# Routing of a top-2 mixture of experts in two parts, the first inside the recurrence that feeds it

## The reference, cut to what matters

```python
x = x + _L0_ffn_ref(_L0_cond_ref(cond_1024, x, ...), ...)   # x: (32, 64, 256)
x = x + _L1_ffn_ref(_L1_cond_ref(x, cond_1024, ...), ...)

def step(h, z_t):                                  # L0_cond: 64 steps in a row
    gate = jax.nn.sigmoid(h @ Wh.T + z_t @ Wz.T + b)
    h_new = jnp.tanh(h * leak + gate * z_t)

gate_hidden = jnp.einsum('nh,erh->ner', x, W_A)    # L0_ffn: 2048 tokens, 8 experts
scores = jnp.sqrt(jnp.sum(gate_hidden * gate_hidden, axis=-1))
topk_scores, topk_idx = jax.lax.top_k(scores, K)   # K = 2
g = jnp.einsum('ner,efr->nef', gate_hidden, W_B)
up = jnp.einsum('nh,efh->nef', x, W_up)
y = jnp.einsum('nef,ehf->neh', jax.nn.silu(g) * up, W_down)
out = jnp.einsum('neh,ne->nh', y, w_full)          # w_full: softmax over the two chosen

h_next = jnp.tanh(xw_t + h_prev @ Wh)              # L1_cond: 64 steps; then L1_ffn: 256 -> 1024 -> 256, quantised
```

## Time and profile before

| | us |
|---|---|
| median of 3 runs | 438.21 (436.7 to 440.9) |
| the profiled execution | 437.36 |
| its span, first to last instruction | 435.6 |
| outside the span | 1.8 |
| PE busy in the span | 341.4 (78%) |
| DVE busy | 260.2 (60%) |
| ACT busy | 212.5 (49%) |
| POOL busy | 247.7 (57%) |

### The profile page before, as it was taken

How to read it: one execution, slowest core, us unless ns; L and a number is a source line. 1 busy time by engine, 2 the same in 40 slices (tenths; PEclk the granted TensorE clock), 3 DMA queues, 4 the chain that set the end, 5 groups by cost and what they waited for, 6 DMA issues and landing times.

```text
span 435.6 us, 12277 instructions
## 1 busy us (share of the span) xinstructions
PE 341.4 (78%) x3791; PEld 230.8 (53%) x3792; DVE 260.2 (60%) x758; ACT 212.5 (49%) x664; POOL 247.7 (57%) x274
## 2 busy tenths in 40 slices
PE   2478777778740179999999999999808999999982
PEld 1345444444410136666666666666507777677741
DVE  5246767767779746853443443343315788989781
ACT  2135555555541124444444445444323787787781
POOL 3579999999002466675445555552046677775231
PEclk9999999999985579999999999999976899999999
DMA  8972365616801012322232232233122122211011
GB/s 210 245 284 75 131 199 214 253 72 204 292 36 60 17 45 72 83 79 74 64 81 78 57 81 81 59 77 66 36 62 74 50 62 77 72 53 56 26 38 36
DMA packets 22525, 42.81 MB, mean 98 GB/s; under 512 B 3986, under 2 KB 14610, under 8 KB 21604
## 3 DMA queue, kind: packets, MB, share of 16 engines
q0 software_dynamic: 6560, 23.17, 18.0%
q1 hardware_dynamic: 15664, 19.31, 13.8%
q10 hardware_dynamic: 276, 0.01, 0.0%
HBM read 28.97 MB, written 13.50 MB: 97 GB/s over the span
## 4 chain that ended last, share of the span: by engine, by line
PE 53%; DVE 16%; DMA 10%; ACT 7%; issue 7%; POOL 2%; SPq 1%; DVEq 0%; POOLq 0%; ACTq 0%
PE bank L916 14%; PE bank L892 12%; DVE bank L1122 5%; PE bank L755 5%; PE bank L762 4%; DMA z<-x_fm 4%; PE bank L882 4%; PE bank L902 4%; DMA z_lo<-y_rows,idx 3%; ACT h_hi L576 2%; ACT bank L574 2%; DMA gate_rows<-ga_s 2%; PE bank L868 2%; PE bank L1020 2%; DVE wrec L1331 1%
## 5 line engine op out<-in xcount | busy, mean ns | idle before, releaser
L1265 DVE TENSOR_TENSOR wrec<-bank,wrec 128x512 f16<-128x512 f32 x39 | 27.0, 691 | 80.8 <-ACT wrec L636 80.6
L755 PE MATMUL bank<-h_hi,wrec_hi 128*128 128x32 f16 x512 | 43.7, 181 | 29.8 <-ACT h_hi L576 28.8
L892 PE MATMUL bank<-wup_s,xt 128*128 x234 | 64.4, 385 | 1.1 <-issue 1.1
L916 PE MATMUL bank<-wdn_s,wrec 128*128 x468 | 62.6, 278 | 3.0 <-ACT wrec L636 1.0
L755 PEld LDWEIGHTS bank<-h_hi,wrec_hi 128*128 128x128 f16 x512 | 34.5, 98 | 56.6 <-ACT h_hi L576 51.5
L478 POOL DMA_INDIRECT xs<-hs_rows,idx x39 | 41.5, 1065 | 31.6 <-POOL idx L474 31.6
L916 PEld LDWEIGHTS bank<-wdn_s,wrec 128*128 128x128 f16 x468 | 41.9, 96 | 17.2 <-issue 7.0
L630 ACT ACTIVATE z_lo<-bank 128x256 f32<-128x256 f32 x39 | 15.0, 384 | 61.6 <-PE bank L916 61.6
L481 POOL DMA_INDIRECT gs<-gate_rows,idx x39 | 38.2, 980 | 11.9 <-issue 11.3
L1122 DVE TENSOR_TENSOR_SCAN bank<-bank,terms 128x128 f32<-128x128 f32 x64 | 27.6, 432 | 28.6 <-ACT bank L574 24.9
L504 POOL DMA_INDIRECT z_lo<-y_rows,idx x32 | 32.3, 1009 | 18.1 <-POOL idx L499 12.2
(11 more groups left out here) (206 smaller groups left out, 922.4 us busy)
## 6 DMA issues: line engine op xcount, KB each, us to landing
y_rows<-z_lo SPq DMA_DIRECT2D x39, 128.0 KB
stage<-wup POOLq DMA_DIRECT2D x2, 2048.0 KB, 11.9
gate_rows<-ga_s SPq DMA_DIRECT2D x16, 256.0 KB, 2.7
stage<-wdn POOLq DMA_DIRECT2D x2, 2048.0 KB, 8.5
stage<-wb SPq DMA_DIRECT2D x2, 1024.0 KB, 13.6
hs_rows<-hs_out SPq DMA_DIRECT2D x16, 128.0 KB, 2.1
stage<-w POOLq DMA_DIRECT2D x2, 1024.0 KB, 7.5
stage<-x_tm POOLq DMA_DIRECT2D x1, 2048.0 KB, 16.0
```

The lines of the kernel that those rows point to most:

```text
L755: mm(fm(par)[:, ft, cols], w[:, m, kt, fcols], h_hi[pp][:, kt, pcols], start=False, stop=True, skip_group_check=True)
L892: ins = mm(bank[4 + par][:, :], xt[par][:, b, kt, :], w_slice(wup_s, a, kt, e), start=kt == 0 and n == 0, stop=kt == KT - 1 and n == 2)
L916: ins = mm(bank[6][:, 0:D], act_t[:, a, ft, :], w_slice(wdn_s, b, ft, e), start=n == 0, stop=n == len(todo) - 1)
L1265: ve.tensor_tensor(act_t[:, 1, :, :].rearrange("p k t -> p (k t)"), bank[(7, 3)[par]][:, :], act_t[:, 0, :, :].rearrange("p k t -> p (k t) ...
```

## The change

The token tiles are split in two parts, tiles 0 to 8 (`EARLY` = 9) and tiles 9 to 15.

The first part is routed during steps of the tiles 11 to 15 of the first recurrence; the last six tiles of it are now written out on PE and DVE. A slot is now known by expert and rank instead of by its place in one list. One-hot rows are made by small DVE instructions of 128 columns (`hots`, lines 1332 and 1333 of the new kernel), two for each token tile and choice, and PE inverts them by 128 x 128 products. Eighteen routed tile halves fill at least 11 slot tiles (`FIRST`), which form the front of the list. Their gathers need only the stored rows of tiles 0 to 8.

The second part is routed by DVE and PE between the expert tiles 0 to 7, and gives the 28 other slot tiles. The slots of the tokens, needed only for the last stage, are worked out at expert tiles 24 to 28. The mixing weights (square root and sigmoid on ACT) move to the last expert tile and behind it.

Gate rows are stored as 64 numbers in f32 instead of a high and a low half in f16. The split into halves is now made after the gather: PE transposes the f32 rows in one more f32 transpose (`transposed_in`), ACT copies both the rows and the high half of the gates (`copy_in`), and DVE forms the low half (`gates_low`). `copy_rows` in the recurrence moves from DVE to ACT, between the sigmoid and the tanh, in two halves. `v`, the scan's output, moves from PSUM bank 6 to bank 2, where `gate` already is.

The load of `x_tm` is issued behind the first two gathers. The constants that POOL makes (`iota`) move to the start of the program, and DVE waits for them before its first step. The work on the quantised weights on DVE is cut into quarters and spread over expert tiles 9 to 12 and 16 to 23. Expert tiles 1 to 16 are written out on PE.

```diff
@@ -23,6 +23,12 @@
 
 
 STILES = 2 * NTOK // P + E - 1
+
+FAR = 1000
+EARLY = 9
+FIRST = 2 * EARLY - E + 1
+CAP = NTOK // P
+COLS = E * CAP
...
+            gather_h(0, 0, EARLY * P)
+            gather_h(1, 1, EARLY * P)
+            pool.dma_start(rows, x_tm.rearrange("(t p) d -> p t d", p=P)).then_inc(s_restage[1], 16)
+            with pool.Fori(1, FIRST // 2) as i:
+                gather_h(2 * i, 0, EARLY * P)
+                gather_h(2 * i + 1, 1, EARLY * P)
+            gather_h(FIRST - 1, 0, EARLY * P)
+            pool.wait_ge(s_route, 2)
             pool.wait_ge(rows_st[0], 16 * TILES // 2)
             pool.wait_ge(rows_st[1], 16 * TILES // 2)
             pool.wait_ge(ga_st[0], 16 * TILES // 2)
             pool.wait_ge(ga_st[1], 16 * TILES // 2)
-
-            def gather_h(j, par):
-                if live(j - 2, STILES):
-                    pool.wait_ge(xt_mm, j - 1)
-                    pool.wait_ge(gh_mm, j - 1)
-                pool.tensor_copy(idx[par][:, 0:2], row_of_slot[:, bass.ds(j, 1), :].rearrange("p a c -> p (a c)")
-                                 ).then_inc(idx_ready, 1)
-                pool.wait_ge(idx_ready, j + 1)
-                pool.sem_inc(waited, 1)
-                pool.indirect_dma_start(out=xs[par][:, :], out_offset=None, in_=hs_dram,
-                                        in_offset=bass.IndirectOffsetOnAxis(ap=idx[par][:, 0:1], axis=0)
-                                        ).then_inc(gathered[par], 16)
-                pool.indirect_dma_start(out=gs[par][:, :], out_offset=None, in_=ga_dram,
-                                        in_offset=bass.IndirectOffsetOnAxis(ap=idx[par][:, 1:2], axis=0)
-                                        ).then_inc(gathered_g[par], 16)
-
-            gather_h(0, 0)
-            gather_h(1, 1)
-            with pool.Fori(1, STILES // 2) as i:
+            gather_h(FIRST, 1)
...
+                    if live(k - 1) and s in (1, 2):
+                        copy_rows(k - 1, 1 - par, s - 1)
...
+            def copy_in(j, par):
+                sc.wait_ge(xt_mm, j + 1)
+                if live(j - 2, STILES):
+                    sc.wait_ge(u_mm, j - 1)
+                    sc.wait_ge(g_mm, j - 1)
+                sc.activation(xt[par][:, :, :, :].rearrange("p a k t -> p (a k t)"), bank[0][:, 0:D].bitcast(F16), ACT.Copy
+                              ).then_inc(xt_ready, 1)
+                sc.activation(gh_s[par][0:R, :], bank[0][0:R, 2 * P:3 * P], ACT.Copy).then_inc(gh_ready, 1)
...
+                    if isinstance(k, int):
+                        if (k, s) == (12, 1):
+                            rank_early()
+                        if (k, s) == (12, 3):
+                            place_of(0, 6)
+                        if (k, s) in ((14, 1), (14, 3), (15, 0)):
+                            inverse_early({(14, 1): 0, (14, 3): 8, (15, 0): 13}[k, s], {(14, 1): 8, (14, 3): 13, (15, 0): 18}[k, s])
+                        if (k, s) == (15, 1):
+                            list_of(0, 6)
...
+            def rank_early():
+                pe.wait_ge(both_ready[0], 1)
+                ranks(6, 0, 0, EARLY).then_inc(rank_mm[0], 1)
...
-            def transposed_h(j, par):
+            def transposed_in(j, par):
                 pe.wait_ge(gathered[par], 8 * (j - par) + 16)
                 if live(j - 1, STILES):
                     pe.wait_ge(xt_ready, j)
+                    pe.wait_ge(gl_ready, j)
                 for c in range(2 * KT):
-                    ins = nc.tensor.transpose(fm16(0, 4)[:, c, :], xs[par][:, c * P:(c + 1) * P], ident[:, :])
-                ins.then_inc(xt_mm, 1)
-
-            def transposed_gates(j, par):
+                    nc.tensor.transpose(fm16(0, 4)[:, c, :], xs[par][:, c * P:(c + 1) * P], ident[:, :])
                 pe.wait_ge(gathered_g[par], 8 * (j - par) + 16)
-                if live(j - 1, STILES):
-                    pe.wait_ge(gh_ready, j)
-                nc.tensor.transpose(fm16(1, 1)[:, 0, :], gs[par][:, :], ident[:, :]).then_inc(gh_mm, 1)
+                nc.tensor.transpose(bank[0][:, 2 * P:3 * P], gs[par][:, :], ident_f[:, :]).then_inc(xt_mm, 1)
...
+            gate_product(0, 0, expert(0))
+            pe.wait_ge(sq_done, 2 * TILES)
+            pe.wait_ge(ga_out, TILES)
+            pe.wait_ge(rows_out, 2 * TILES)
             up(0, 0, 0, expert(0))
...
+            for m in range(8):
+                expert = experts()
+                expert_tile(2 * m + 1, 1, expert, 0)
+                if m == 0:
+                    rank_late()
+                if m == 2:
+                    inverse_late()
+                expert_tile(2 * m + 2, 0, expert, 1, None if 2 * m + 3 == FIRST - 2 else 2 * m + 3)
+                if m == 0:
+                    place_of(1, 1)
...
-                    if live(k - 2) and s == 1:
-                        gates_low(k - 2, par, 0)
-                    if live(k - 1) and s == 2:
-                        copy_rows(k - 1, 1 - par)
+                    if isinstance(k, int):
+                        if k == 11 and s >= 1:
+                            pick_early((0, 2, 4)[s - 1])
+                        if (k, s) == (12, 1):
+                            loads(0, ea)
+                        if (k, s) == (12, 3):
+                            slot_ranks(0, 1)
+                        if (k, s) == (13, 1):
+                            place_tiles(0, 6)
+                        if (k, s) == (13, 2):
+                            hots(0, 1, 3)
+                        if (k, s) == (13, 3):
+                            hots(0, 5, 6)
+                        if k == 14 and s >= 1:
+                            hots(0, (8, 11, 14)[s - 1], (9, 12, 16)[s - 1])
+                        if (k, s) == (15, 1):
+                            copy_inverse_early()
+                        if (k, s) == (15, 2):
+                            list_rows(0, 6)
...
+            def loads(c, of):
+                link(ve.tensor_reduce(load[:, :], both[:, :, of], AXX, ALU.add))
+                ve.tensor_copy(load_of[c][:, :, :], load[:, :].unsqueeze(2).broadcast_to([P, E, CAP])
+                               ).then_inc(both_ready[c], 1)
...
+            def hots(p, first, end):
+                x, at = ((early, 0), (late, EARLY))[p]
+                for n in range(first, end):
+                    c, t = n % 2, n // 2
+                    ve.tensor_scalar(x[0][:, c, t, :], iota_col[:, :], col_of[:, c, at + t:at + t + 1], None, ALU.is_equal)
+                    ve.tensor_scalar(x[1][:, c, t, :], iota_slot[:, :], row_in[:, c, at + t:at + t + 1],
+                                     token_id[:, at + t:at + t + 1], ALU.is_equal, ALU.mult).then_inc(hot_ready[p], 1)
...
+            def copy_inverse_early():
+                dve.wait_ge(inv_mm[0], 1)
+                ve.tensor_copy(inv_s[:, :], bank[6][:, 256:384]).then_inc(inv_ready[0], 1)
...
+            def gates_low(j, par):
+                dve.wait_ge(gh_ready, j + 1)
+                ve.tensor_tensor(gh_s[par][R:P, :], bank[0][0:R, 2 * P:3 * P], gh_s[par][0:R, :], ALU.subtract
+                                 ).then_inc(gl_ready, 1)
...
+            for t in range(TILES - 3, TILES):
+                sum_squares(t, 0)
+                sum_squares(t, 1)
+            gates_low(0, 0)
+            gates_low(1, 1)
+            dve.wait_ge(score_done, 2 * TILES)
+            pick_late(0)
+
+            expert_tile(0, 0)
+            pick_late(1)
+            dve.sem_inc(s_top, 1)
+            count_both(la)
+            loads(1, la)
+            expert_tile(1, 1)
+            for part in range(3):
+                slot_ranks(1, part)
+            expert_tile(2, 0)
+            hots(1, 0, 6)
+            expert_tile(3, 1)
+            place_tiles(1, 1)
+            hots(1, 6, 11)
+            expert_tile(4, 0)
+            hots(1, 11, 2 * late_n)
+            expert_tile(5, 1)
+            add_inverse_late()
```

More of the change, by code:

```diff
@@ new lines, in ranks @@
+            def ranks(b, c, first, n):
+                o = bank[b][:, 0:E * n].rearrange("p (e t) -> p e t", e=E)
+                chosen = both[:, :, first:first + n]
+                mm(o, before[:, :], chosen, start=True, stop=False, skip_group_check=True)
+                for d in range(1, n):
+                    ins = mm(o[:, :, d:n], ones[:, :], chosen[:, :, 0:n - d], start=False, stop=c == 0 and d == n - 1,
+                             skip_group_check=True)
+                if c == 1:
+                    mm(o, ones[:, :], load_of[0][:, :, 0:n], start=False, stop=True, skip_group_check=True)
+                for a in range(c + 1):
+                    ins = mm(bank[b][:, 128:129], load_of[a][:, :, :].rearrange("p e k -> p (e k)"), ones[:, 0:1],
+                             start=a == 0, stop=a == c)
+                return ins
@@ new lines, in rank_early, with rank_late, place_of, inverse @@
+            def rank_early():
+                pe.wait_ge(both_ready[0], 1)
```

(12 more changed lines are left out.)

565 lines of the change are left out of this document (332 added, 233 removed).

## The result

| | before | after |
|---|---|---|
| median of 7 runs | 438.68 us (436.7 to 440.9) | 434.0 us (433.0 to 435.04) |
| ratio, 95% interval | | 0.988 (0.986 to 0.990) |
| the profiled execution, its span | 437.36, 435.6 | 433.0, 431.1 |
| mean granted clock of PE | 0.943 | 0.936 |

The change gains 1.2%, 4.5 us of the span. Forecast were 14.4, and 434.0 lies 5 us above the upper end of the forecast range, 429. Four points in both profiles show where the rest went: the start of the last scan (before line 1122, after line 1214), the end of the first and of the last `down` (before line 916, after line 986), and the end of the span.

A forecast was written before the change was run, and what follows sets the result against it. PE bounds the expert tiles at 4.0 us each, a DVE chain the routing gap before them. -21.0 (gap) + 1.2 (clock) + 1.7 (recurrence) + 2.1 + 1.6 (expert tiles) = -14.4 us: median 423.8, range 419.5 to 429.

The forecast's parts named there:

- (b): Recurrence, tile 11: the choices, two linked DVE instructions in each of six holes, overrun them; +0.45 us.
- (a): Recurrence, step (12,1): `rank_early` on PE waits for `loads` from DVE and delays the next step's products; +0.55 us.
- (c): Recurrence, tile 12: ranks and columns on DVE take 0.66 us in one hole; +0.2 us.
- (d): Recurrence: PE's inverse products, eight and five, stand behind other work; +0.15 us.
- (f): Recurrence: 36 one-hot instructions on DVE, at most four in a hole, at 0.13 us each; +0.15 us.
- (e): Recurrence, step (15,2): the words, four small DVE instructions, take 0.76 us in a hole of 0.55; +0.2 us.
- no blocking by `x_tm`: Rival at the handover: the `x_tm` load does not hold up slot tile 2's gathers; 420.0 us, chance 0.2.
- the 1.2 for the clock: Handover: the idle wait before slot tile 2 can lower PE's clock, putting further matmuls at half rate; +1.2 us.
- the f32 transpose: Expert tiles: gates go through an f32 transpose on PE, 0.055 us more for each of 38 tiles; +2.1 us.
- Gathers held up by one-hots: Rival at slot tiles 2 to 4: one-hots on DVE delay POOL's gathers, PE 2 us late; 425.8 us, chance 0.1.
- the slower rival: Expert tiles: the gates' longer way through ACT and DVE becomes a tile's bound; 442.5 us at 0.5 a tile, chance 0.03.

The follow-up runs named there:

- e2: New kernel with the intermediate results of the choices for tiles 0 to 8 in PSUM bank 6 instead of SBUF; 429.7 us, ratio 0.981.
- e6: e4 with half of the one-hots of tiles 0 to 8 made by POOL, and one pair on DVE in each of nine holes; 421.7 us, ratio 0.959.
- e5: e4 with ACT's copies of slot tile 0 ahead of the silu table load and DVE's late choices before and between the first low halves; 422.1 us.
- e4: New kernel with the edits of e1 and e2, and POOL's splits of `wrec` waiting for the last one-hot of tiles 0 to 8; 424.4 us, ratio 0.971.
- e1: New kernel with the load of `x_tm` issued at its old place, behind the loads of `w`; 429.3 us, ratio 0.980.
- e3: New kernel with POOL waiting before its third split of `W_down` until the choices for tiles 0 to 8 and their loads are made; 437.2 us, ratio 0.997.
- e7: e4 with the changed handover order of e5 and half of the one-hots on POOL as in e6; 420.3 us, ratio 0.957.

## Why the prediction was wrong

The sum had the right sign, and the gain in the gap came as it said. The step that failed is (b), "The choices of tile 11: six holes with two linked instructions each, 0.54 to 0.62 us in 0.5 or 0.55": +0.45 predicted, +7.3 measured. Its price was that of DVE's instructions by themselves, and that was 1.0 (the three steps in e2). The other 6.3 are the wait for POOL's splits, which the sum put at nothing. What runs beside the choices was not looked at, though the page of the kernel before shows it, in POOL's row of the forty slices (10.9 us each, busy share in tenths):

```profile
POOL 3579999999002466675445555552046677775231
```

The slices from 33 to 109 us are full: those are the splits, up to the DMA issue at 102.51, and tile 11 lies at 90 to 97. The prediction asked about POOL only for the gathers, and of the section that is named next it used only the rule on the two-port mode. The Trainium skill, page "SBUF — State Buffer", section "Who interferes with whom", says that a DVE instruction with two SBUF inputs contends with a GpSimd instruction that reads SBUF, and that the second to issue is blocked until the first ends. The trace agrees: 1.20, 1.67 and 2.95 us for 0.22 us of work, and 0.21 to 0.24 with one input in PSUM (e2). By that rule each of the eight two-input instructions of the choices could have waited for a split of up to 4.1 us, which as a rival would have been worth more than all others. None of the instructions that the recurrence had before has two inputs in SBUF, so there the trace of before could not show the wait. But in its last stage it shows. Timeline of the kernel before:

```profile
356.42 1.12 POOL L519 TENSOR_SCALAR z<-z_hi,quant 128x1024 f16<-128x1024 f32 x1
356.70 0.91 DVE L1389 TENSOR_TENSOR h_lo<-h,h_hi 128x64 f16<-128x64 f32 x1
...
358.70 0.22 DVE L1389 TENSOR_TENSOR h_lo<-h,h_hi 128x64 f16<-128x64 f32 x1
...
361.71 1.12 POOL L519 TENSOR_SCALAR z<-z_hi,quant 128x1024 f16<-128x1024 f32 x1 [0.21 <-issue]
361.85 1.13 DVE L1331 TENSOR_SCALAR wrec<-stage 128x256 f16<-128x256 f32 x1
```

Line 1389 has two inputs in SBUF and takes 0.21 to 0.26 us in 56 of its 64 instructions. In the other eight, each beside POOL, it takes 0.45 to 0.91; the one shown ends at 357.61, POOL's at 357.54. Line 1331 has one input and takes 1.13 instead of 0.28. A mean that is far above the minimum (277 and 207 ns for line 1389) is the sign to look for.

The other terms of the recurrence, by the step table:

- (a) The rank counts of (12,1): +0.55 predicted, +0.38 in (12,2). The wait is the one described.
- (c) Ranks and columns: +0.2 predicted, +0.21 in (13,0).
- (d) and (f), PE's inverse and the one-hots: +0.3 predicted, +2.2 measured, (13,1) to (15,0). One instruction was taken at 0.13; they follow at 0.16 and 0.22. The hole's length was right: in e6, with one pair in a hole, only (13,2), which also places the tiles, is above 1.67 (1.74). (14,2), where PE also has eight products of the inverse, is 2.45 here and in e5, 1.92 in e4 and 1.67 in e6, so what is put down to PE is not a fixed size.
- (e) The words: +0.2 predicted, +0.17 in (15,3).
- `v` in the bank of `gate` and `copy_rows` on ACT: 0 predicted and 0 measured, 1.66 a step up to tile 10. The constants at the start: 0 predicted, +0.44 measured, which is less than the spread of this stretch from profile to profile (2.0 us), so no cost is shown. The first scan is 1.6 later (0.4 to 1.6 in the eight profiles), and the wait for z takes most of it back, as predicted. 0.76 of the 1.6 is the same wait for POOL, of an instruction with one input that takes 0.24 in e4:

```profile
10.32 1.04 POOL L400 TENSOR_SCALAR wa_s<-stage 128x1024 f16<-128x1024 f32 x1 [1.16 <-DMA stage<-wa]
...
10.41 1.00 DVE L1204 TENSOR_SCALAR col_e<-col_p,col_k 128x128 f16<-128x128 f16 x1
```

The gap. From the last tanh to the first `W_B` product 8.0 us were predicted and 8.0 came out, with the parts in the predicted order. From there to the wanted rows of tile 2, landed: 7.7 predicted, 8.75 measured; the load took 11.1 us from its issue instead of 9.5. The wait was 4.53 instead of 2.6, e1 shows its cause, and *no blocking by `x_tm`* falls. From those rows to the end of the first `down`: 6.25 predicted, with the 1.2 for the clock, and 6.27 measured, but not for the reason given. (The parts that the prediction lists there, from 138.4, give 141.95 and not its 142.3; the transposes of tile 2 are not in the list.) The clock did not fall at the wait for tile 2. It was 0.50 from 140.5 on, 5 us before that wait began, stayed there through it, and rose at 154. In e1, where PE waits 1.25 us, the clock is 0.50 until 149, and the same stretch takes 6.07. So the long wait cost some 0.2 by the clock, and the half clock was there without it.

The expert tiles. +3.7 predicted, +1.3 measured. Two tiles take 8.05 us before and 8.07 after in the steady part, so the f32 transpose costs 0.01 a tile and not 0.055: 2.1 was too much by some 1.7. The late routing costs some 0.9: from the end of the first `down` to PE's transposes of the activation of tile 5 (line 974; 902 before) it is 18.28 us instead of 17.34. *Gathers held up by one-hots* did not happen: after tile 2, PE waited for no gather. What shows is the reverse: at 166.15 a late one-hot takes 0.53 instead of 0.30 and ends at 166.68, as POOL's issue of a gather does at 166.67. Nor did the slower rival come, as a bound of every tile; its wait, for `gl_ready`, is 1.25 us at one place, ahead of the transposes of tile 2, in the five runs with `x_tm` early.

The tail. 0 predicted, +2.3 measured, and this is not settled. 1.9 of it stands in one step: in the timeline of DVE, the first two rows of the new kernel, the last of the kernel before at the same place.

```profile
329.24 0.48 DVE L1543 SCALAR_TENSOR_TENSOR wrec<-z_lo,mixw,stage 128x256 f32<-128x256 f32 x1 [2.60 <-DMA z_lo<-y_rows,idx]
329.76 0.48 DVE L1548 SCALAR_TENSOR_TENSOR stage<-z_lo,mixw,wrec 128x256 f32<-128x256 f32 x1
```

```profile
334.08 0.48 DVE L1318 SCALAR_TENSOR_TENSOR wrec<-z_lo,mixw,stage 128x256 f32<-128x256 f32 x1 [0.81 <-DMA z_lo<-y_rows,idx]
```

Both gathers were issued at the same distance from the last `down` (15.3 and 15.1 us), and this one landed 4.4 us behind its issue instead of 2.7. In all eight profiles of the new kernel and its variants DVE waits 2.2 to 2.6 us for this gather, also with `x_tm` early. The mixing weights are ready some 18 us before. Why this gather and not another remains open; no run was aimed at it.

Against the forecast of the span, term by term: +6.8 (b), +1.9 (d and f), +1.1 (the gap), +2.3 (tail), +0.4 (start), -0.2 (a), -2.4 (expert tiles), together the 9.9 us by which the span missed the sum. That the expert tiles (-2.4) and the tail (+2.3) cancel is luck.

## What to carry to other kernels

Work that is put into the holes of a waiting engine is priced with what the other engines do in the same microseconds, instruction by instruction: for DVE, whether its inputs lie in SBUF and what POOL does there. Compare the mean and the minimum of an instruction in the trace at hand: a wait of this kind stands in its duration. Where both must run, put one input into PSUM; moving POOL's block (e3) only chooses another victim. A DMA that nobody needs soon belongs ahead of the gathers (e1), not between two of them; another queue was not tried. And a hole is filled by what follows in issue, 0.38 for a pair here, one pair and not two.

## What the runs showed of the hardware that was not expected

- A DVE instruction with two SBUF inputs waits for POOL's instructions with one input (1.67 in the new kernel, 0.91 in the kernel before) and with two (2.95). With one SBUF input it depends on the kind. A `tensor_reduce` did not wait (0.28 at 96.44, beside a split with two inputs). A `tensor_scalar` waited beside two inputs (2.60 us for 18 columns, 0.90 for a one-hot of 0.24, both in e3) and beside one (1.13 in the kernel before, 1.00 in the new one), but not at 109.42 in e6, 0.26 inside POOL's 0.59. The Trainium skill, page and section as above, describes the one-input case as an exclusive lock either way when DVE is in a two-port mode. The waits of `tensor_scalar` agree with that; the one-hot of e6 ran on, and why is open.
- Step (11,2) takes 2.26 to 2.28 us in all of e2 to e7, where no choice waits for POOL. In e4 DVE is idle there for 0.55 us ahead of a scan whose sigmoid had ended. It is not explained. With 0.6 us it is more than half of the 1.0 that the choices cost by themselves.
- A load of 2 MB on POOL's queue took 11.1 us from issue to landing while the DMA engines were busy to 0.90. The gather issued behind it at 140.87 landed at 150.09, 0.3 us after it.
